# Products of the identity with itself where TensorE waits: attention with distances, both routers and the end of the encoder

## The reference, cut to what matters

```
x = x + L0_xattn(layernorm(x), ctx)      # cross attention, 16 heads of 64
x = x + L0_attn(layernorm(x))            # Performer encoder: kernel features, feed-forward of 512, two layer norms
x = x + L0_ffn(layernorm(x))             # 8 experts, the 2 best per row, and a shared expert
x = x + L1_xattn(layernorm(x), ctx)      # cross attention, 16 heads of 8
x = x + L1_attn(layernorm(x))            # attention with distances: softmax(q k / sqrt(8) - slope |i - j|) v, 16 heads of 8
x = x + L1_ffn(layernorm(x))             # 32 experts, 4 of 8 groups, then the 8 best per row, and a shared expert
```

## Time and profile before

| | |
|---|---|
| median of three runs | 2778.41 us (2778.01 to 2785.14) |
| profiled execution | 2784.49 us |
| its span | 2782.7 us |
| granted TensorE clock, mean over the span | 0.949 |
| PE busy | 2604.0 us (94%), 39151 matmuls |
| PE weight loads busy | 2214.1 us (80%) |
| DVE busy | 1640.8 us (59%) |
| ACT busy | 1478.0 us (53%) |
| POOL busy | 1026.6 us (37%) |

### The profile page before, as it was taken

The page is one execution under the profiler, slowest core; times in us unless marked ns, Lnnn a source line. Parts: engine busy times, 40 slices in busy tenths (PEclk is TensorE's granted clock), DMA queues, the critical chain, the costliest instruction groups (busy, mean ns, idle before and its releaser), DMA issues. The chain is left out here.

```text
span 2782.7 us, 94896 instructions
## 1 busy us (share of the span) xinstructions
PE 2604.0 (94%) x39151; PEld 2214.1 (80%) x39151; DVE 1640.8 (59%) x3266; ACT 1478.0 (53%) x4035; POOL 1026.6 (37%) x1208
## 2 busy tenths in 40 slices
PE   6999999999999999998599987999999898899998
PEld 5888888888778888886488985777777677899997
DVE  3555555555575666665555544777777555555553
ACT  3454545555535666665544435777777433444443
POOL 2333333443330000004344444666666323344443
PEclk9999999999999999998699997999999767799999
DMA  6322222222000000000100002011000100000001
GB/s 208 112 85 85 96 97 85 85 91 86 30 1 1 0 0 0 0 0 1 52 1 0 0 0 73 23 28 28 23 28 23 50 0 1 1 0 0 0 0 31
DMA packets 32692, 99.28 MB, mean 36 GB/s; under 512 B 4309, under 2 KB 18265, under 8 KB 27737
## 3 DMA queue, kind: packets, MB, share of 16 engines
q1 hardware_dynamic: 32602, 98.01, 10.6%
HBM read 93.80 MB, written 4.19 MB: 35 GB/s over the span
## 5 line engine op out<-in xcount | busy, mean ns | idle before, releaser
L566 POOL TENSOR_TENSOR l_probs<-l_probs,l_rden 128x1024 f32<-128x1024 f32 x128 | 242.2, 1893 | 429.1 <-DVE l_rden L424 429.1
L508 ACT ACTIVATE l_probs<-ps,l_nmax 128x257 f32<-128x257 f32 x512 | 236.0, 474 | 226.4 <-DVE l_nmax L418 226.4
L973 POOL TENSOR_TENSOR l_probs<-l_probs,l_rden 128x1024 f32<-128x1024 f32 x128 | 242.3, 1893 | 172.3 <-DVE l_rden L843 172.3
L418 DVE TENSOR_REDUCE l_nmax<-ps 128x2 f32<-128x514 f32 x256 | 165.5, 688 | 217.3 <-PE ps L303 217.3
L913 ACT ACTIVATE l_probs<-ps,l_nmax 128x257 f32<-128x257 f32 x512 | 235.9, 474 | 57.9 <-DVE l_nmax L837 57.7
L2717 POOL TENSOR_TENSOR m_hh<-m_hh,m_comb_t 128x512 f32<-128x512 f32 (+2 forms) x160 | 143.2, 895 | 224.0 <-DVE m_hh L2643 224.0
L303 PE MATMUL ps<-l_ctxQ,l_q 32*128 32x257 f32 x3072 | 202.6, 392 | 7.1 <-ACT l_probs L508 6.4
L837 DVE TENSOR_REDUCE l_nmax<-ps 128x2 f32<-128x514 f32 x256 | 165.4, 688 | 66.0 <-PE ps L743 62.1
L2643 DVE TENSOR_TENSOR m_hh<-ps,m_sg 128x512 f32<-128x512 f32 (+2 forms) x160 | 95.6, 598 | 180.2 <-ACT m_sg L2485 180.0
L848 DVE COPY l_pT<-ps 128x512 f32<-128x512 f32 x256 | 164.9, 686 | 53.9 <-PE ps L752 49.7
L343 PE MATMUL ps<-l_pT,l_ctxK 128*32 128x128 f32 x6144 | 194.3, 275 | 0.8 <-DVE l_pT L461 0.8
(11 more groups left out here) (362 smaller groups left out, 6832.2 us busy)
## 6 DMA issues: line engine op xcount, KB each, us to landing
l_ctxQ<-in_ctx_q SPq DMA_DIRECT2D x32, 1542.0 KB, 6.5
l_ctxT<-in_ctx_t SPq DMA_DIRECT2D x32, 385.5 KB, 3.3
l_ctxK<-in_ctx_k SPq DMA_DIRECT2D x32, 384.0 KB, 3.1
x<-in_x SPq DMA_DIRECT2D x4, 512.0 KB, 7.4
scratch<-l_W SPq DMA_DIRECT2D x2, 1024.0 KB, 4.8
l_last_w<-scratch SPq DMA_DIRECT2D x32, 64.0 KB
out_x<-x SPq DMA_DIRECT2D x1, 2048.0 KB, 8.7
m_w<-in_m_w SPq DMA_DIRECT2D x3, 512.0 KB, 4.7
```

The lines of the kernel that those rows point to most:

```text
L418: nc.vector.tensor_reduce(nmax[:, par, 2 * half:2 * half + 2], ps[:, S_B + 2 * half:S_B + 2 * half + 2, 0:NK], AX.X, ALU.max, negate=True) ...
L508: nc.scalar.activation(probs[:, par, hg, :], ps[:, S_B + hg, 0:NK], ACT.Exp, bias=nmax[:, par, hg:hg + 1], accum_out=den[:, par, hg:hg + 1 ...
L566: nc.gpsimd.tensor_tensor(pr, pr, rden[:, b, :, None].to_broadcast([P, HG, NK - 1]), ALU.mult).then_inc(norm_ok, 1)
L973: nc.gpsimd.tensor_tensor(pr, pr, rden[:, b, :, None].to_broadcast([P, HG, K_W]), ALU.mult).then_inc(norm_ok, 1)
```

## The change

A helper issues n products of the identity with itself into a bank of PSUM that nobody reads at that time. It is called at four places: 8 products at the end of the encoder, once seven of eight groups are added; in router 0, 8 at its start, one ahead of each group's transposes and 40 behind the last group; in the attention with distances, two per tile between the keys and queries and the value product; in router 1, 8 at its start and one ahead of each group.

```diff
@@ -1602,6 +1602,11 @@
             block = end.enter_context(nc.Block())
 
+            @block.tensor
+            def _(pe):
+                pe.wait_ge(x_ok, NG - 1)
+                keep_clock(nc, k, 7, 8)
+
             @block.scalar
...
+def keep_clock(nc, k, bank, n):
+    for _ in range(n):
+        nc.tensor.matmul(k.ps[:, bank, 0:P], k.ident[:, :], k.ident[:, :], start=True, stop=True)
...
@@ -1812,8 +1822,10 @@
 
+            keep_clock(nc, k, 7, 8)
             pe.wait_ge(g_in, 32)
             for g in range(NG):
+                keep_clock(nc, k, 7, 1)
                 if g > 1:
                     pe.wait_ge(xf_ok, g - 1)
                 pe.wait_ge(xv_ok, g + 1)
@@ -1824,6 +1836,7 @@
                 if g:
                     route(g - 1)
             route(NG - 1)
+            keep_clock(nc, k, 7, 40)
             pe.wait_ge(st, 10)
             pe.wait_ge(zero_ok, 1)
@@ -2215,6 +2228,9 @@
                 if has(2):
                     keys_queries(t + 2, j)
+                if has(-1):
+                    keep_clock(nc, k, O_B, 2)
+                if has(2):
                     value(t + 2, j)
                 if has(-1):
                     pe.wait_ge(at_ok, t)
```

## The result

| | before | the change |
|---|---|---|
| median of 20 runs | 2780.89 us | 2771.72 us |
| lowest run | 2768.05 us | 2765.30 us |
| profiled execution | 2784.49 us | 2768.20 us |
| granted clock, mean | 0.949 | 0.967 |
| PE busy | 2604.0 us | 2603.1 us |

The ratio is 0.9965 with a 95% interval from 0.9951 to 0.9979: about 10 us faster, a little over what one measurement can tell. The forecast was 2754 (2740 to 2770): right in sign, too large, and the median lies above the range. A few executions took 3.0 to 7.5 ms, at a mean granted clock of 0.64 to 0.80 where it is on record; ratios, means and spreads leave them out.

A forecast was written before the change was run, and what follows sets the result against it. PE was taken to bound these stages, at a clock it mostly doesn't get. Terms -20.2 + 0.5 + 0.7 - 5.8 - 0.7 = -25.5 us, from 2778.4 or 2784.5, gave 2752.9 to 2759.0: forecast 2754 us, range 2740 to 2770.

The forecast's parts named there:

- That the products raise the clock, and that the wait for ACT hides them: Attention: two products (0.46 us) fit the 0.47 us wait at full clock; tiles go from 5.77 to 3.96 us. Chance 0.78.
- The products don't count: Rival, all places: the clock stays as it is and each product costs half-clock time; +27 us, 2805 us; chance 0.07.
- Too few in the attention: Rival: two products per tile leave the attention's clock alternating, half as much time cold; about 2765 us; chance 0.15.
- The attention's term: Loop of the attention with distances: tiles at half clock run at full, less start and occasional falls; -20.2 us.
- Of this I take back two tiles at the start: Attention's loop: products begin with tile 1 and the clock must first rise; 5.1 us of the gain taken back.
- the 62% at half clock: Attention's loop: 62% of 142 us, 88 us, at half clock; at full they shrink to 60.4, 27.3 us less.
- The tail: Last four tiles behind the attention's loop: ever fewer products, half clock expected; +0.5 us.
- Encoder's end: End of the encoder: 8 products make PE last at the barrier; +0.7 us, zero if the clock rises within them.
- Router 0: Router 0: groups at full clock save 5.3 us, the stretch behind the 40 products 0.5; together -5.8 us.
- With 16 products nearly in a row the clock should be full when the groups begin: Start of router 0: full clock for the groups, each 1.65 us instead of 2.45; -5.3 us.
- the 0.5 forecast for what is behind them: Expansion behind router 0's 40 products: the clock may fall again, so only part of its 2.7 us gained; -0.5 us.
- Router 1: Router 1: groups gain 1.7 us net after a cold start; about 1 goes back if the clock falls behind; -0.7 us.

The follow-up runs named there:

- attention only: The change with only its two products per tile in the attention, none in routers or encoder: 2773.52 us, ratio 0.9963 against before.
- four per tile: Against the kernel before, only products in the attention with distances, four per tile instead of the change's two: ratio 1.0002.
- attention and the 40: The change without the 8 + 8 + 8 and the one per group, run twice: 2765.89 us, 0.9945, and 2766.23 us, 0.9932 against before.
- router 0 held: The change with two products per group and 70 behind them in router 0, router 1 as before; twice: 2765.05 us, 0.9936, and 2762.94 us, 0.9920.
- the change with the small ones: The change plus 40 products of 32x32 by 8 behind its 40 large ones: 2769.51 us, ratio 0.9916 against before.
- two per group: The change with two products instead of one ahead of each group's transposes in both routers: ratio 0.9992 against before.
- the one from the first tile on: Against the kernel before, only the attention's two products per tile, but in every step from the first, not from tile 1 on: ratio 0.9994.
- the 40 small ones: The kernel before plus only 40 products of 32x32 by 8 behind router 0's groups, in place of 40 large ones: 2774.08 us, ratio 0.9958.

## Why the prediction was right in sign and wrong in size

**That the products raise the clock, and that the wait for ACT hides them** was right. The attention runs at 1.00 from 2232 on, with steps of 3.95 and 4.47 us. Eight further profiles bear it out: the second of the change, attention only, four per tile, and two each of attention and the 40 and of router 0 held, and the change with the small ones. In all nine the clock stays full from the tenth of the 27 steps on; in each of the nine profiles without products in the tiles it falls again there. The jump's pause is 0.34 to 0.39 us at full clock in both kinds, so it doesn't explain that. Not tested was the control that the 40 got, tiny products in the attention's tiles, and two kernels go the other way: two per group had one step of 5.30 us in the loop, and the one from the first tile on had half clock in it to the end. "The products don't count" fell. "Too few in the attention" holds for the first steps and not for the loop, though the time came out nearer its 2765 than the forecast's 2754.

The page that advises against idle gaps between bursts (the Trainium skill, TensorE: Matmul & The Clock Gate, Why this matters for your kernels) doesn't settle this stage. Before, PE was idle for 8.4 of the 142 us at a clock of 0.69, never for more than 1.3 us at once, and in the change for 142 - 130.1 = 11.9 us at 0.91: little idle time at half clock does not bring the clock back. At full clock the products do leave less of it. Over 70 us of the loop, the 40 small ones (no product in the tiles) and then attention only:

```profile
2260.00:2330.00 70.00, 62.34 (x3302) 52.85 (x3303) 48.48 (x115) 30.95 (x100) 23.29 (x32) 0.98 0.00 0
...
2260.00:2330.00 70.00, 66.95 (x3489) 59.99 (x3484) 48.80 (x118) 30.44 (x97) 24.07 (x34) 1.00 0.00 0
```

PE was idle for 7.7 us there without them and for 3.1 with them, never for more than 0.39 at once. Without them 4.8 us of it lay ahead of the value product, the wait for ACT, and with them none; what is left is the jump's pause. Whether it is the filled waits or the kind of work that holds the clock, no run separates.

**The attention's term** was the step that failed, in two places. First, "Of this I take back two tiles at the start": it was five. The first five steps of the change are 6.60, 7.09, 7.19, 6.34 and 5.13, together 32.4 us against 28.7 before, at half clock for the most part and with two pauses in them:

```profile
2215.39 0.41 PE L2194 MATMUL ps<-al_kbd,al_kq 32*32 32x128 f32 x3 [2.14 <-issue]
...
2220.77 0.49 PE L2214 MATMUL ps<-al_va,al_pT 32*32 32x9 f32 x19 [1.12 <-issue]
```

From the sixth on, 22 steps took 92.5 us instead of 113.0, which is 20.5 less. Taken together the loop fell from 141.7 to 124.9, -16.8 where the text had -20.2. Two small errors of the text lie in that too: 88 - 60.4 is 27.6, not 27.3, and every second step of the loop holds the jump and goes from 6.17 to 4.50 us only, so that 88 us shrink by some 25.6. Second, and larger, the 62% at half clock, read from one execution, were taken for the kernel's. The mean of the three profiles of before is 138.7 us, so the change gains 12.6 with its own mean of 126.1 over two profiles, and the attention alone, timed, gave 9. The text saw that the median lay 6 us below the profiled execution and that this might be the alternation, and then took off too little for it.

**The tail:** +0.3 (22.05 against 21.7 in the means), forecast +0.5. **Encoder's end:** +0.9, forecast +0.7.

**Router 0:** forecast -5.8. "With 16 products nearly in a row the clock should be full when the groups begin" held, and a group took 1.6 us. But the full clock was counted on for all the groups: it fell at the fifth, and the groups behind it paid 0.54 us each for their product. First to last transpose stayed at 16.9. The 40 products then did more than the 0.5 forecast for what is behind them: they fit into the wait, the clock was full by 1391, and the expansion fell from 9.6 in the mean to 6.9. Both together, with the encoder's end: -1.9 against the mean of before (25.7 + 17.0 + 15.3 + 9.6 = 67.6 became 65.7), not -5.1.

**Router 1:** forecast -0.7. The entry +0.9, the groups -2.2 in one profile and +1.5 in the other, and behind them the clock was down again at 2371, as feared; router 1's experts took 375.6 and 375.8, which is what two of the three profiles of before had as well. Nothing or a loss. The stages' means add up to -13.7 us, and the means of the profiled executions differ by 13.3 (2784.5 of three, 2771.2 of two), so no large term is missing from this account.

**What no step had** is that added instructions shift the pauses of those behind them. The 64 ahead of the attention left the first pauses where they were; its own two per tile moved those further on (2215.39 above), and what that cost or gave was not measured apart. With 40 or 104 ahead the ratios are lower. That the change's 64 are just one period, which leaves the first places alone, is chance: nothing in the prediction looked at it, and with 72 ahead (two per group) the gain was gone.

## What to carry to other kernels

Where a stage alternates between two clocks, take its length from several executions before sizing a gain from it: here the loop of one profile each gave 16.8 us, and the means of three and two gave 12.6. When instructions are added in front of a long list, run a control with as many instructions that do next to nothing: 40 tiny products gave most of what was first put down to 40 large ones. Halves of a change that don't add up are a sign that such a control is needed. Fill a wait with as many products as it holds and no more; products between router 0's groups were paid for in full (0.54 us each) when the clock fell in spite of them.

## What the runs showed of the hardware

- The same program differs by almost 40 us between executions (2768 to 2808 for before, over 133 of them), and the mean granted clock goes with it (correlation -0.76 to -0.93).
- PE pauses of 0.2 to 2.4 us without a releaser sit at fixed places of the instruction list. They repeat every 128 matmuls with their weight loads: 64 products more ahead of them leave the places as they are; 24, 40, 72, 102 and 104 move them by twice their number, less multiples of 128. The jump of the attention's loop holds one too, 0.34 to 0.39 us in most kernels and 0.62 in the one with two per group and the one from the first tile on: 4.47 or 4.72 us for a step with the same work.
- In router 0, one 128x128 product per group did not hold full clock in any of six profiles. Two did in two profiles of three.
- In the attention with distances, two 128x128 products per tile kept the clock at 1.00 from the tenth step on in eight profiles of ten, and four per tile in one of one; without them it fell again in nine of nine.
